# The last batch norm of a graph kernel: statistics of its second half put ahead of the first half's scale, both square roots ahead of the affines, and x put into the output banks behind the last product

## The reference

```
h = jnp.maximum(_layernorm(x, axis=-1), 0.0)
h = einsum('nd,df->nf', h, W);  agg = segment_sum(A_values * h[col], row)
h = agg + bias
mean = jnp.mean(h, axis=0);  var = jnp.mean(jnp.square(h - mean), axis=0)
h = (h - mean) * jax.lax.rsqrt(var + BN_EPS) * gamma + beta
return x + relu(h)
```

## Time and profile before

| | us |
|---|---|
| median of 3 runs | 114.09 |
| the profiled execution's own time | 114.17 |
| its span, first to last instruction | 112.4 |
| TensorE busy (share of span) | 100.6 (89%) |
| VectorE busy | 92.5 (82%) |
| ScalarE busy | 57.4 (51%) |

### The profile page before, as it was taken

How to read it: one execution, slowest core, us unless ns; L and a number is a source line. 1 busy time by engine, 2 the same in 40 slices (tenths; PEclk the granted TensorE clock), 3 DMA queues, 4 the chain that set the end, 5 groups by cost and what they waited for, 6 DMA issues and landing times.

```text
span 112.4 us, 2688 instructions
## 1 busy us (share of the span) xinstructions
PE 100.6 (89%) x1040; PEld 92.4 (82%) x1040; DVE 92.5 (82%) x266; ACT 57.4 (51%) x143; POOL 19.8 (18%) x27
## 2 busy tenths in 40 slices
PE   0398999799999999999899999998999998999930
PEld 0335898687998899989899999997999997999720
DVE  2399999999999999999986699767989989437950
ACT  2497999997897690312807035506233145141630
POOL 7100000000000099410093700660000000000000
PEclk9999999999999999999999999999999999999997
DMA  1867810000200000000153000000000000000044
GB/s 42 239 207 181 281 34 0 0 6 3 92 7 0 6 9 6 0 0 3 14 172 99 0 0 0 0 6 0 0 6 0 0 0 0 0 0 6 0 109 121
DMA packets 5401, 4.63 MB, mean 41 GB/s; under 512 B 555, under 2 KB 5386, under 8 KB 5386
## 3 DMA queue, kind: packets, MB, share of 16 engines
q1 hardware_dynamic: 4460, 3.68, 11.5%
q10 hardware_dynamic: 926, 0.75, 2.4%
HBM read 3.79 MB, written 0.64 MB: 39 GB/s over the span
## 4 chain that ended last, share of the span: by engine, by line
PE 36%; issue 24%; DVE 21%; ACT 7%; POOL 5%; DMA 3%; DVEq 0%; SPq 0%; POOLq 0%; ACTq 0%
PE bank L1125 8%; PE bank L1127 7%; PE bank L1126 7%; PE bank L1375 7%; DMA edge_rows_i<-in_dst_dram 3%; DVE stats L534 3%; DVE pre L741 3%; DVE x_in L674 2%; POOL parts L480 2%; POOL own L489 2%; PE bank L1415 2%; PE bank L1188 2%; DVE h_lo L751 2%; DVE pre L745 1%; PE bank L1275 1%
## 5 line engine op out<-in xcount | busy, mean ns | idle before, releaser
L581 DVE TENSOR_SCALAR src_hot<-node_id,edge_cols 125x626 f16<-125x626 f16 x77 | 23.5, 380 | 0.0
L1275 PEld LDWEIGHTS bank<-dst_hot,src_hot 125*128 125x128 f16 x505 | 19.0, 98 | 3.3 <-DVE src_hot L581 1.7
L1275 PE MATMUL bank<-dst_hot,src_hot 125*128 125x84 f16 (+6 forms) x505 | 20.4, 195 | 1.4 <-DVE src_hot L581 0.9
L1375 PE MATMUL bank<-counts,u_lo 125*128 125x312 f32 (+1 forms) x60 | 16.3, 308 | 0.0
L1051 ACT ACTIVATE h_hi<-pre 128x312 fp32r<-128x312 f32 (+1 forms) x12 | 5.6, 466 | 18.1 <-DVE pre L745 18.1
L480 POOL TENSOR_TENSOR parts<-parts 125x625 f32<-125x625 f32 x5 | 6.4, 1297 | 43.1 <-DVE src_hot L581 35.9
L1375 PE MATMUL bank<-counts,u_hi 125*128 125x312 f32 (+1 forms) x48 | 14.0, 307 | 0.0
L1375 PEld LDWEIGHTS bank<-counts,u_lo 125*128 125x128 f32 x60 | 10.9, 189 | 0.0
L994 ACT ACTIVATE parts<-bank 125x250 f32<-125x250 f32 x25 | 10.2, 411 | 0.0
L1375 PEld LDWEIGHTS bank<-counts,u_hi 125*128 125x128 f32 x48 | 9.1, 189 | 0.0
L918 ACT ACTIVATE counts<-bank 125x125 fp32r<-125x125 f32 (+1 forms) x25 | 7.4, 297 | 2.0 <-PE bank L1275 2.0
(11 more groups left out here) (143 smaller groups left out, 252.8 us busy)
## 6 DMA issues: line engine op xcount, KB each, us to landing
raw<-in_L_gnn_W_dram SPq DMA_DIRECT2D x3, 512.0 KB, 6.5
x_in<-in_x_dram ACTq DMA_DIRECT2D x1, 560.0 KB
raw<-in_L_gnn_Wf_dram SPq DMA_DIRECT2D x1, 512.0 KB, 3.8
out_dram<-x_in SPq DMA_DIRECT2D x2, 168.0 KB
wf<-in_L_gnn_Wf_dram SPq DMA_DIRECT2D x1, 256.0 KB, 7.8
raw<-in_L_gnn_Wf_dram SPq DMA_DIRECT2D x1, 256.0 KB, 2.8
raw<-in_L_gnn_W_dram SPq DMA_DIRECT2D x1, 256.0 KB, 3.5
out_dram<-x_in SPq DMA_DIRECT2D x2, 112.0 KB
```

What stands on the lines that cost most here:

```text
L581: dve.tensor_scalar(src_hot[:, t % RING, 0:IDS], node_id[:, 0:IDS], edge_cols[:, 0, t:t + 1], None, ALU.is_equal).then_inc(src_hot_vector, 1)
L1275: return pe.matmul(built[s][:, :, n0:n0 + n], src_hot[:, t % RING, BLK * s:BLK * s + P], dst_hot[:, c, :, j // 2, c0:c0 + n, j % 2], start ...
L1375: ins = pe.matmul(bank[KF * h + f][:, 0:e - a], u[:, k, P * f:P * (f + 1)], counts[0:BLK, k, a:e], start=False, stop=(k == NB - 1 and u is ...
```

## The change

Three lists of instructions change, and no instruction is added or dropped.

```diff
 VectorE
-            for f in range(KF):
-                for h in range(2):
-                    moments_of_agg(f, h)
-                variance_of_agg(f)
-                centre(f)
-                affine(f)
+            moments_of_agg(0, 0)
+            moments_of_agg(0, 1)
+            variance_of_agg(0)
+            centre(0)
+            moments_of_agg(1, 0)
+            affine(0)
+            moments_of_agg(1, 1)
+            variance_of_agg(1)
+            centre(1)
+            affine(1)
 ScalarE
             root(rstd[:, 0:1], moments[:, 0, 1:2])
+            root(rstd[:, 1:2], moments[:, 1, 1:2])
             act.wait_ge(scale_ready, 1)
             act.wait_ge(bn_ready, 1)
             affine(0, 0)
             affine(0, 1)
-            root(rstd[:, 1:2], moments[:, 1, 1:2])
-            copy_out(0)
             act.wait_ge(scale_ready, 2)
             act.wait_ge(bn_ready, 2)
             affine(1, 1)
+            copy_out(0)
             copy_out(1)
 TensorE
-            put_x(0)
             pe.wait_ge(*LO_W4)
             for q, (f, h) in enumerate(AGG):
...
                 ins.then_inc(filled, 1)
+            put_x(0)
             put_x(1)
```

## The result

The changed kernel takes 114.72 us in the median of six runs (114.59 to 114.94), the kernel before 114.23 in six (113.9 to 114.41). The ratio is 1.0047 with a 95% interval of 1.0034 to 1.0061: slower by 0.49 us, clear of the noise and just inside the 0.5% (0.57 us) that the prediction named as the edge of what counts as a change.

The account below looks back on a forecast made before the run. Taken as the bound: the output transfer at the end, its start set by ScalarE's copies as much as VectorE's additions. 114.17 + 0.55 (transfer) = 114.72, less 0.08 for the median 114.64, rounded to 114.6; range 114.1 to 115.1.

Parts of the forecast that it names:

- x behind the products: TensorE, put_x(0) moved behind the products: the products start 0.01 to 0.10 us earlier, 0.05 taken.
- Statistics ahead of affine(0): VectorE, one statistic moved ahead of affine(0): bounds 0.04 us gained to 0.05 lost, value 0.
- Root ahead of both affines: ScalarE, root(1) ahead of the affines: root gains 0.03 us by this edit, first affine at 106.13, last addition 0.06 late.
- The DMA issues: SyncE's queue: four issues in a row from 108.07, the last at 109.55, 0.23 us late.
- The transfer: Output writes at the end: 512,000 bytes to go from group 1's start at 109.63, ending 0.55 us later.
- backlog: Main case, output writes at the end: bytes still to be moved set the end, +0.3 to +0.8 us, chance 0.50.
- only the last issue counts: Rival, output writes at the end: the end moves by group 3's issue, +0.23 us, to 114.3; chance 0.20.
- All of the delay goes through: Rival, output writes: the end moves by group 1's 0.83 up to group 0's 1.25 us, 114.9 to 115.3; chance 0.17.
- The gain through VectorE's chain: Rival, VectorE's run from 105.7 to 107.8: faster by 0.1 to 0.45 us, 113.65 to 114.0; chance 0.13.

Follow-up runs that it names:

- the merged DMA: The changed kernel, only that groups 0 and 1 are written by one DMA per queue once both are copied out; ratio to the kernel before 1.0095.

## Why the prediction was right

Forecast 114.6 with a slowdown of 0.55 us on the profiled execution; measured 114.72, with 0.49 between the medians. The mechanism is the one forecast: ScalarE stands at the second root, its copies come late, and with them the output. The closeness of the number is in part luck, as the steps below show: two errors in the transfer took each other off, and the 0.55 of the profiled pair has 0.14 in it that isn't the change's. The steps:

- **x behind the products.** Booked -0.05, with 0.01 to 0.10 as bounds. Measured 0.00: the first product starts at 101.45, aligned 101.31, exactly the old time. The wait for the second low part costs what put_x took. The bound from L907's row (0.14 from VectorE to TensorE) was the right one, and I had taken the middle.
- **Statistics ahead of affine(0).** Booked 0. The second variance starts at 105.74 aligned, as before. There was no wait for the root to fill. What I said less clearly than the runs do: in the old order of ScalarE this edit, with TensorE's, costs 0.4%.
- **Root ahead of both affines.** First affine predicted 106.13, measured 106.18 aligned; copies 107.66 and 108.25, measured 107.68 and 108.30; end of the additions 109.36, measured 109.40. The gain at L907 was 0.03 instead of 0.08, since TensorE gave nothing. The forecast start of the additions, 108.47, was near (108.51) without a reason given: it stands 0.41 behind the first matmul of that turning, while the rows that it was taken from have 0.50 (107.91 to 108.41). In the changed kernel it was 0.42 (108.23 to 108.65).
- **The DMA issues.** Predicted 108.07, 108.76, 109.16 and 109.55; measured, aligned, 108.09, 108.81, 109.22 and 109.73. The last one is 0.18 later than I said: I gave issues 0.36 each as in the earlier trace rows, but those had 0.14 us or more of room between them; right behind one another they take 0.47 and 0.55.
- **The transfer.** I let the end be set by group 1's start and 512,000 bytes, at a rate between 210 and 256 GB/s, and let the tail stay. The rate is 229. The dense part ends 0.76 late aligned instead of 0.55, and the tail, 0.3 instead of 0.6, gives most of the difference back: 0.46. The DMA engines also weren't near a share of 1.0 from the first byte on, as I expected: between group 0 and the backlog, from 109.50 to 110.10, it was 0.61. That a backlog can set the end was shown by the merged DMA, not by the profile of the change, in which both fit: the last issue is 0.41 late and the time 0.49.

Of the rivals, "only the last issue counts" at +0.23 failed in its number, as the last issue itself came 0.41 late; as a mechanism it failed at the merged DMA, which ended later with the same last issue, and it isn't excluded as a part of the changed kernel's cost. The figures that the prediction sets beside it from the Trainium skill (DMA: Bandwidth & Descriptors, "Anatomy of one DMA — SWDGE (gpsimd) path") are a fit for DMAs issued by GpSimd. The DMAs of this kernel are issued by SyncE and ScalarE, and there was a backlog, 133,000 bytes in front of the last group, where that rate would have left none. "All of the delay goes through" overstates it, since group 0's 1.25 us don't count in the changed kernel: without group 0 it is no faster. The gain through VectorE's chain did not come, as the turning for f = 1 found TensorE busy; it started at 108.09 aligned, behind f = 0, against 107.91.

Open is also how much of the cost in the kernel with VectorE's and TensorE's edits is the last addition and how much the transfer; additions and all four issues moved together there, by 0.39. It costs nearly what the full change costs, with the same last issue (109.71) but group 1 issued 0.48 earlier than there, so group 1's start alone doesn't set the end either.

## What to carry to other kernels

An engine that has nothing on the chain of waits can still set when output transfers begin; before putting a wait at the head of its list, add up what is behind it. A root or other small step is worth moving ahead only by the time it really waits, here 0.04 us, not by its own length. And two lists that feed each other have to be costed together: each of the two halves of this change cost 0.4% to 0.5% alone, and both together no more.

## What the runs showed of the hardware

- A DMA issue of 112 partitions on SyncE's queue took 0.32 to 0.37 us when it started 0.14 us or more behind the end of the one before, and 0.46 to 0.57 when it started at most 0.07 behind it. Behind a first DMA of 320,000 bytes in all the third issue took 0.84:

```profile
109.95 0.84 SPq L451 DMA_DIRECT2D out_dram<-x_in  x1
```

- Writes in pieces of 512 bytes from one core went out at 227 to 239 GB/s while backed up: 229 over 2.2 us in the changed kernel, 227 over 2.8 in the merged one, 235 over 2.1 without group 0, 239 over 2.6 with group 0 issued late.
- A second semaphore wait ahead of L907 went with 0.30 us of idle on VectorE, although that semaphore had been counted up before the first one. Ahead of L815, which has two waits too, VectorE idled only 0.04 (94.44 to 94.48 in the kernel before). What makes this one dear is open; the two waits in the other order were not tried.
